# Router parts at the ends of beats, a block list by coded steps, and the last attention beats filled with the shared block

## The chip, the cores and the metric

The kernel runs on one core of a Trainium2 chip. Its five engines are PE (TensorE, matrix products into PSUM banks), DVE (VectorE), ACT (ScalarE), POOL (GpSimd) and SP (SyncE, which here only issues DMAs). They run their own instruction streams in order and wait for each other by semaphores. The metric is device time in microseconds (us), the median of a few executions. PE's clock has two levels here, 1.2 and 2.4 GHz; the profile gives the granted clock as a share of the full one.

## The reference

```python
xn = layernorm(x)                                    # x: 16 batches x 256 tokens x 128
kv = xn @ W_kv; kv = kv * rsqrt(mean(kv**2) + 1e-6) * g_kv;  qc = xn @ W_q
q = concat(heads(qc @ W_qdec), rope(heads(qc @ W_qrope)))    # 16 heads, 8 + 32 wide
k = concat(heads(kv @ W_kdec), rope(heads(xn @ W_krope)))
attn = softmax(where(causal, q @ k.T / sqrt(40), -inf)) @ heads(kv @ W_vdec)
w, e = top2(softmax(xn @ Wg));  w = w / (sum(w) + 1e-9)      # 8 experts
routed = sum_k w_k * (silu(xn @ W1[e_k] + b1[e_k]) @ W2[e_k] + b2[e_k])
shared = silu(xn @ Ws1 + bs1) @ Ws2 + bs2
out = x + attn @ W_o + routed + 0.1 * shared
```

All products are taken in fp32 accuracy: operands are split into a rounded high part and a low rest, and two or three products are summed.

## The kernel before

**Attention.** The 16 batches with 16 heads each make NG = 64 groups, numbered g: four groups for a batch, and in each the query or key side of projections and four heads. The order of everything is written by hand as beats t from -7 to LAST = 71 of four steps s each; (t, s) names a step. In beat t, PE makes the projection of group t (in step 0, `project`); DVE multiplies it by the rope table (L1149, L1156, L1157) in step 1; POOL adds and takes low parts (L761, L766); ACT copies (L945). PE turns parts of group t - 1 and t - 2 (`turn_parted`, L1578) and makes scores for the row maximum of one head in each step (`scores_for_max`, L1593 to L1596), which DVE reduces (`head_max`, L1164). A ring of three PSUM banks (`B_BANKS`) is shared by these scores and turned parts, so PE can't run more than about a step ahead of L1164. The maxima of a group's four heads are turned (L1605), split in a high part (ACT, L928) and a low one (DVE, L1182), and SP copies both into two rows of the operand QK (`place_maxima`, two DMAs of 4 KB, L588) in step (g + 4, 3). Three steps on, the head scores of the group begin (`head_scores`, L1615 to L1618; group 62 in (67, 2), group 63 in (68, 2)); ACT takes exponentials (L914) and PE sums values (`group_values`, L1629, L1632). Each pair of groups is copied out (ACT, L994), turned (L1640), divided by its row sums (DVE, L1190, L1194) into oT; each batch's oT is turned (L1649), copied (ACT, L957), multiplied by W_o (L1660) and added to xres (DVE, L1452).

**Router.** For each quarter q of the tokens, `router(q, part)` runs ten parts on DVE, part 0 to 9, at (16 q + beat, step) of the tables SPREAD (q = 0 to 2) and DENSE (q = 3). Part 4 is L1232 and L1235 on 512 elements for each partition, part 9 begins with L1257. `list_blocks` is a generator: each `next` at a step of LIST_AT issues one piece. It makes the list of the 23 blocks (NB) of 512 routed rows, an expert number and a first row for each (`block_e`, `block_row`, semaphore s_tab), the return places of the tokens' results (`out_at`, s_back) and the chosen biases (`bsel`, s_bsel). POOL scatters the rows to DRAM (L820) up to beat 66.

**Passes.** PASSES are two passes of the shared expert over 512 tokens, 23 routed blocks, then six more shared ones. In pass m PE turns the block (`turn_block`, L1720), makes the hidden layer in four chunks of three products (`hidden`, L1738), and the second layer (`expert_out`, L1802, L1806), and turns the result (L1815). ACT applies Silu (`activate`, L1029) and makes high parts (L1035), DVE low ones (L1480). SP loads weights (L641) and rows (L633) two passes ahead. POOL gathers results (L871) in the late passes and DVE adds them (L1505). Before the first pass SP issues four loads of 512 KB for the shared expert at (66, 0) (`load_shared`).

## Time and profile before

| | |
|---|---|
| median of 3 runs | 718.98 us (717.71 to 720.65) |
| the profiled execution | 720.41 us; its span 718.7 us |
| busy: PE, DVE, ACT, POOL | 652.2, 537.8, 528.6, 430.5 us |
| mean granted PE clock | 0.969 |
| attention beats 0 to 63 | 17.25 to about 465 us |
| last beats | to about 505 us |
| passes | second layer of pass 0 at 518.91 us, the end at 718.7 us |

The span is from the first to the last instruction; the profiled execution's own time is 1.7 us longer. A busy share says how long an engine worked, not that it set the end.

### The profile page before, as it was taken

Reading aid. Unit: us, or ns where it says so; the run is one execution under the profiler, and the core shown is the slowest. Engines: PE = TensorE matmul, PEld = TensorE weight load, DVE = VectorE, ACT = ScalarE, POOL = GpSimd, SP = SyncE. Lnnn points to the kernel's source line nnn. Section 1 sums busy time; section 2 is a strip of 40 time slices with the busy share of each in tenths; the row PEclk is TensorE's granted clock in tenths of the full one; section 3 lists DMA queues with packets and bytes.
Section 4 is the critical chain, followed back from the end, with each engine's and each line's share of the span. In section 5 each row is a group of like instructions: output and inputs, shape, how many; then the busy total and the mean of one; then the engine's idle time right before and its main releaser. Section 6 shows DMA issues by size and latency. Waiting matters only on the chain.

```text
span 718.7 us, 16421 instructions
## 1 busy us (share of the span) xinstructions
PE 652.2 (91%) x5478; PEld 560.2 (78%) x5478; DVE 537.8 (75%) x1327; ACT 528.6 (74%) x1071; POOL 430.5 (60%) x440
## 2 busy tenths in 40 slices
PE   2699989899979999998999999976899999999994
PEld 1588878878868878887888888864688888888883
DVE  6387777686786787777778688788377777788895
ACT  3478868778868778886887888853577777777772
POOL 6677767788887878877687685840000000655773
PEclk9999999999998999998999999988699999999998
DMA  7203113032130321201210000235137777889753
GB/s 194 79 2 105 61 47 105 8 115 65 54 112 7 116 65 54 91 29 42 77 47 32 33 13 21 87 104 204 59 131 222 250 245 247 274 276 291 222 148 85
DMA packets 51953, 79.37 MB, mean 110 GB/s; under 512 B 6289, under 2 KB 31870, under 8 KB 51870
## 3 DMA queue, kind: packets, MB, share of 16 engines
q1 hardware_dynamic: 47198, 69.23, 30.0%
q0 software_dynamic: 4096, 8.40, 4.2%
q8 instruction: 45, 0.74, 0.4%
q10 hardware_dynamic: 576, 0.69, 0.3%
q14 instruction: 38, 0.31, 0.2%
HBM read 47.82 MB, written 29.88 MB: 108 GB/s over the span
## 4 chain that ended last, share of the span: by engine, by line
PE 59%; DVE 14%; POOL 11%; ACT 8%; issue 7%; DMA 1%; POOLq 0%; DVEq 0%; ACTq 0%; SPq 0%
PE bank L1578 6%; PE bank L1802 6%; PE projections L1738 5%; PE bank L1738 5%; PE bank L1629 4%; PE bank L1615 3%; PE bank L1806 3%; POOL QK L871 3%; PE bank L1618 3%; PE bank L1593 2%; PE bank L1596 2%; ACT heads_parted L945 2%; DVE mx L1164 2%; POOL heads_parted L766 2%; ACT QK L920 2%
## 5 line engine op out<-in xcount | busy, mean ns | idle before, releaser
L920 ACT ACTIVATE QK<-bank 120x512 fp32r<-120x512 f32 x256 | 154.9, 606 | 32.7 <-PE bank L1578 27.1
L914 ACT ACTIVATE prob<-bank 128x384 f32<-128x384 f32 x256 | 128.3, 501 | 56.6 <-PE bank L1618 56.4
L871 POOL DMA_INDIRECT QK<-expert_outs,out_at x64 | 67.2, 1050 | 159.4 <-DMA expert_outs<-prob 140.4
L1164 DVE TENSOR_REDUCE mx<-bank 128x3 f32<-128x384 f32 x256 | 140.9, 550 | 22.9 <-PE bank L1596 21.7
L1578 PE MATMUL bank<-identr,heads_parted 128*120 128x128 f32 x1024 | 138.1, 261 | 17.7 <-DVE mx L1164 11.6
L1578 PEld LDWEIGHTS bank<-identr,heads_parted 128*120 128x120 f32 x1024 | 106.6, 141 | 24.6 <-DVE mx L1164 13.6
L766 POOL TENSOR_TENSOR heads_parted<-rot,heads_parted 128x640 fp32r<-128x640 f32 x64 | 101.2, 1581 | 38.1 <-ACT heads_parted L945 37.5
L1480 DVE TENSOR_TENSOR QK<-vaug,QK 128x512 fp32r<-128x512 f32 x124 | 86.4, 698 | 41.6 <-ACT QK L1035 39.2
L761 POOL TENSOR_TENSOR rot<-rot,t 128x512 f32<-128x512 f32 x64 | 82.1, 1283 | 33.7 <-DVE t L1157 33.6
L1593 PE MATMUL bank<-QK 120*128 120x256 f32 x256 | 94.8, 370 | 4.8 <-DVE mx L1164 3.0
L1615 PE MATMUL bank<-QK 122*128 122x256 f32 x256 | 90.7, 355 | 3.5 <-DMA QK<-mT 3.4
L945 ACT ACTIVATE heads_parted<-rot 128x1280 fp32r<-128x1280 f32 x64 | 82.3, 1286 | 1.6 <-POOL rot L761 1.5
L820 POOL DMA_INDIRECT expert_rows<-xn,place_of x64 | 65.5, 1023 | 25.2 <-issue 9.9
L1149 DVE TENSOR_TENSOR rot<-projections,rope_table 128x640 f32<-128x640 f32 x64 | 52.6, 822 | 36.0 <-PE projections L1566 28.5
L1618 PE MATMUL bank<-identb,mask_qk 128*128 128x256 bf16 x256 | 74.3, 290 | 0.0
L1596 PE MATMUL bank<-mask_qk,identb 128*128 128x256 bf16 x256 | 74.3, 290 | 0.0
L1594 PE MATMUL bank<-QK 120*128 120x128 f32 x256 | 57.8, 226 | 0.0
L1616 PE MATMUL bank<-QK 122*128 122x128 f32 x256 | 57.7, 225 | 0.0
L1593 PEld LDWEIGHTS bank<-QK 120*128 120x128 f32 x256 | 52.8, 206 | 6.2 <-DVE mx L1164 3.3
L1615 PEld LDWEIGHTS bank<-QK 122*128 122x128 f32 x256 | 49.5, 193 | 6.0 <-DMA QK<-mT 3.7
L1594 PEld LDWEIGHTS bank<-QK 120*128 120x128 f32 x256 | 50.5, 197 | 0.0
L1616 PEld LDWEIGHTS bank<-QK 122*128 122x128 f32 x256 | 50.2, 196 | 0.0
(226 smaller groups left out, 1582.0 us busy)
## 6 DMA issues: line engine op xcount, KB each, us to landing
wb<-weight_parts SPq DMA_DIRECT2D x46, 512.0 KB, 4.8
weight_parts<-wb SPq DMA_DIRECT2D x18, 512.0 KB, 3.4
rot<-expert_rows SPq DMA_DIRECT2D x23, 256.0 KB, 4.3
expert_outs<-prob SPq DMA_DIRECT2D x23, 256.0 KB, 4.8
xn<-in_L_ffn_W SPq DMA_DIRECT2D x16, 256.0 KB, 4.0
xn_parts<-wb SPq DMA_DIRECT2D x16, 256.0 KB, 2.8
heads_parted<-xn_parts SPq DMA_DIRECT2D x8, 512.0 KB, 4.5
expert_rows<-zeros SPq DMA_DIRECT2D x15, 256.0 KB, 2.8
```

The lines of the kernel that those rows point to most:

```text
L766: nc.gpsimd.tensor_tensor(low_of(g), rotated(g), high_of(g)[:, :, 0:D], ALU.subtract).then_inc(s_lo, 1)
L871: nc.gpsimd.indirect_dma_start(out=gy[:, t, k, :], out_offset=None, in_=outs_d[0:READY[q] * SLOTS, :], in_offset=bass.IndirectOffsetOnAxis ...
L914: act_f(prob[:, g % 2 * HG + n, :], ST_PS[n % 2][:, 0:3 * P], ACT.Exp, scale=SCALE).then_inc(s_exp, 1)
L920: act_f(stacked(g, i), B_PS[bank_of(k)][0:KQ, :].rearrange("p (h t) -> p h t", h=HG), ACT.Copy)\
L945: act_f(high_of(g).rearrange("p m (a d) -> p m a d", a=2), rotated(g).unsqueeze(2).to_broadcast([P, NT * PH, 2, D]), ACT.Copy).then_inc(s_ ...
L1164: V.tensor_reduce(mx[:, g % 2, 0:3, n], B_PS[bank_of(k)][:, 0:3 * P].rearrange("p (a c) -> p a c", a=3), AX.X, ALU.max, negate=True).then_ ...
L1578: ins = nc.tensor.transpose(B_PS[bank_of(k)][0:KQ, n * P:(n + 1) * P].bitcast(F32R), parted(g)[:, j * PH + 2 * n + odd, :], identr[:, :])
L1593: mm(ps[:, 0:T], q[:, P:T], kk, start=True, stop=False, skip_group_check=True)
L1594: mm(ps[:, T:3 * P], q[:, 0:P], kk[:, 0:P], start=False, stop=False, skip_group_check=True)
L1615: mm(ps[:, P:3 * P], k[:, 0:P], q, start=True, stop=False, skip_group_check=True)
L1616: mm(ps[:, 0:P], k[:, P:T], q[:, P:T], start=False, stop=False, skip_group_check=True)
L1618: mm(diag, mask_qk[:, :], identb[:, :].unsqueeze(1).to_broadcast([P, 2, P]), start=False, stop=True, skip_group_check=True).then_inc(s_st, 1)
```

## The change

- SPREAD puts seven of the ten router parts at the last step of a beat. Part 4 moves from (12, 0) to (13, 3), counted from the quarter's first beat, part 9 from (19, 0) to (18, 3).
- The block list no longer selects a segment by equality and sums two products. Expert number times 65536 plus shift is one code for each segment; the steps between the codes of neighbours are summed over all segments that a block has passed, and the expert number is the count of multiples of 65536 that the sum reaches. LIST_AT has 10 entries for 21, from (61, 3) to (68, 3).
- The return places come last in the generator and are issued in passes 3 to 10 (BACK_AT). The biases come ahead of them.
- The shared block's first hidden layer stands in four places of the last beats, (68, 0), (68, 1), (69, 1), (69, 2), and two chunks of the second pass behind the beats. The values of group 62 move from (69, 0) to (68, 1). The last batch's turning and output product leave the beats and use bank 7, with copies and addition on DVE; the last pair's copy moves from ACT to DVE.
- ACT calls Silu on two elements behind its last beat and then waits for the last values.
- SP issues the loads of weights for the first two routed blocks behind all maxima, and after each block's rows.

```diff
--- before.py
+++ after.py
@@ -117,7 +117,9 @@
-    if s == 0 and group(t - 7) and (t - 7) % 2 == 0:
+    if (t, s) == (LAST - 3, 1):
+        return NG - 2
+    if s == 0 and group(t - 7) and (t - 7) % 2 == 0 and t - 7 < NG - 2:
...
@@ -181,11 +183,12 @@
-SPREAD = ((8, 3), (10, 3), (11, 0), (11, 3), (12, 0), (12, 2), (14, 3), (16, 3), (18, 3), (19, 0))
+SPREAD = ((8, 3), (10, 3), (11, 3), (12, 3), (13, 3), (14, 2), (14, 3), (16, 3), (17, 3), (18, 3))
-LIST_AT = ((62, 3), (63, 3), (64, 0), (64, 1), (64, 2), (64, 3), (65, 0), (65, 1), (65, 2), (65, 3), (66, 0), (66, 1),
-           (66, 2), (66, 3), (67, 0), (67, 1), (67, 2), (68, 0), (68, 1), (68, 2), (69, 2))
+LIST_AT = ((61, 3), (62, 3), (63, 3), (64, 3), (65, 3), (66, 3), (67, 1), (67, 3), (68, 1), (68, 3))
+BACK_AT = (3, 4, 5, 6, 7, 8, 9, 10)
+CODE = 65536
...
@@ -662,13 +668,9 @@
-                if t in (67, 68) and s == 0:
-                    if t == 67:
-                        sp.wait_ge(s_tab, 1)
-                        sp.wait_ge(s_pfill, NG)
-                    for part in range(2):
-                        load_weights(t - 67, part)
+            sp.wait_ge(s_tab, 1)
+            sp.wait_ge(s_pfill, NG)
...
@@ -676,6 +678,8 @@
+                for part in range(2):
+                    load_weights(r_, part)
...
@@ -951,7 +955,7 @@
-                if s == 2 and out_batch(t) is not None:
+                if s == 2 and out_batch(t) in range(B - 1):
...
@@ -987,7 +991,7 @@
-                if s == 3 and pair_at(t) is not None:
+                if s == 3 and pair_at(t) in range(NG // 2 - 1):
...
@@ -1041,6 +1045,8 @@
+            act_f(warm[:, :], mhalf[:, :], ACT.Silu).then_inc(s_table, 1)
+            sc.wait_ge(s_pv, NG)
...
@@ -1336,31 +1344,44 @@
+                steps.add(V.scalar_tensor_tensor(out=coded, in0=expert_no[:, :], scalar=float(CODE), in1=shift, op0=ALU.mult,
+                                                 op1=ALU.add))
+                steps.add(V.tensor_tensor(leap, coded[:, 1:SEGS + 1], coded[:, 0:SEGS], ALU.subtract))
-                steps.add(V.tensor_tensor(sel[:, :, 0:SEGS], by_block(block_no, SEGS), each(flat2(end), SEGS), ALU.is_ge))
+                steps.add(V.tensor_tensor(sel, by_block(block_no, SEGS), each(flat2(end), SEGS), ALU.is_ge))
-                steps.add(V.tensor_reduce(seg, sel[:, :, 0:SEGS], AX.X, ALU.add))
+                steps.add(V.tensor_tensor(sel, sel, each(leap, SEGS), ALU.mult))
-                steps.add(V.tensor_tensor(sel, by_block(seg, SEGS + 1), each(seg_no[:, :], SEGS + 1), ALU.is_equal))
+                steps.add(V.tensor_reduce(code, sel, AX.X, ALU.add))
-                steps.add(V.tensor_tensor(val, sel, each(expert_no[:, :], SEGS + 1), ALU.mult))
+                steps.add(V.scalar_tensor_tensor(out=code, in0=block_no, scalar=float(SLOTS), in1=code, op0=ALU.mult, op1=ALU.add))
+                steps.add(V.tensor_tensor(bound, by_block(code, E - 1), each(code_of[:, :], E - 1), ALU.is_ge))
+                steps.add(V.tensor_reduce(no, bound, AX.X, ALU.add))
+                steps.add(V.tensor_copy(block_e[:, :], no))
+                steps.add(V.scalar_tensor_tensor(out=row, in0=no, scalar=-float(CODE), in1=code, op0=ALU.mult, op1=ALU.add))
+                steps.add(V.tensor_tensor(chosen, by_block(no, E), each(seg_no[:, 0:E], E), ALU.is_equal))
+                V.tensor_copy(block_row[:, :], row).then_inc(s_tab, 1)
-                steps.add(V.tensor_tensor(sel, sel, each(shift, SEGS + 1), ALU.mult))
+                steps.add(V.tensor_tensor(parts, chosen.unsqueeze(2).to_broadcast([P, NB, FC, E]),
+                                          bias[:, 0:E * FC].rearrange("p (e c) -> p c e", c=FC).unsqueeze(1)
+                                          .to_broadcast([P, NB, FC, E]), ALU.mult))
-                steps.add(V.tensor_reduce(no, val, AX.X, ALU.add))
-                steps.add(V.tensor_reduce(row, sel, AX.X, ALU.add))
-                steps.add(V.tensor_copy(block_e[:, :], no))
-                steps.add(V.scalar_tensor_tensor(out=row, in0=block_no, scalar=float(SLOTS), in1=row, op0=ALU.mult, op1=ALU.add))
-                steps.add(V.tensor_tensor(chosen, by_block(no, E), each(seg_no[:, 0:E], E), ALU.is_equal))
-                V.tensor_copy(block_row[:, :], row).then_inc(s_tab, 1)
+                steps.add(V.tensor_tensor(second, chosen, each(bias[:, NE * FC:NE * FC + E], E), ALU.mult))
+                dve.wait_ge(s_sc[GROUPS - 1], 16 * 2 * GT)
+                steps.add(V.tensor_reduce(bsel[:, :, 0:FC], parts, AX.X, ALU.add))
+                V.tensor_reduce(bsel[:, :, FC:FC + 1], second.unsqueeze(2), AX.X, ALU.add).then_inc(s_bsel, 1)
...
@@ -1439,12 +1450,16 @@
+                if s == 3 and pair_at(t) == NG // 2 - 1:
+                    dve.wait_ge(s_pv, NG)
+                    dve.wait_ge(s_bk, NG // 2 - 1)
+                    V.tensor_copy(heads_out[:, :], PV_PS[:, 0:T]).then_inc(s_ev, 1)
-                if s == 0 and added_batch(t) is not None:
+                if s == 0 and added_batch(t) in range(B - 1):
...
@@ -1458,6 +1473,11 @@
+            dve.wait_ge(s_lfill, 1)
+            V.tensor_copy(oT[:, :], banks[7][:, 0:T]).then_inc(s_lread, 1)
+            dve.wait_ge(s_lfill, 2)
+            V.tensor_tensor(xres[:, TILES - NT:TILES, :], banks[7][:, T:2 * T].rearrange("p (j c) -> p j c", j=NT),
+                            xres[:, TILES - NT:TILES, :], ALU.add).then_inc(s_lread, 1)
...
@@ -1515,6 +1535,8 @@
+                if m in BACK_AT:
+                    next(listing, None)
...
@@ -1758,6 +1780,8 @@
+                if (t, s) == (LAST - 3, 1):
+                    hidden(0, (1,))
...
@@ -1767,7 +1791,7 @@
-                if s == 1 and out_batch(t) is not None:
+                if s == 1 and out_batch(t) in range(B - 1):
...
@@ -1778,17 +1802,28 @@
-                if s == 3 and out_batch(t) is not None:
+                if s == 3 and out_batch(t) in range(B - 1):
-                if (t, s) == (LAST - 2, 3):
+                if (t, s) == (LAST - 3, 0):
-                    hidden(0, range(0, 2))
-            ring_empty(pe)
-            hidden(0, range(2, FC))
-            pe.wait_ge(s_exp, H * B)
+                    hidden(0, (0,))
+                if (t, s) == (LAST - 2, 1):
+                    ring_empty(pe)
+                    hidden(0, (2,))
+                if (t, s) == (LAST - 2, 2):
+                    hidden(0, (3,))
+            hidden(1, (0,))
+            for j in range(NT):
+                ins = nc.tensor.transpose(banks[7][:, j * P:(j + 1) * P], oT[:, j * P:(j + 1) * P], ident[:, :])
+            ins.then_inc(s_lfill, 1)
+            hidden(1, (1,))
+            pe.wait_ge(s_lread, 1)
+            for j in range(NT):
+                ins = mm(banks[7][:, T + j * P:T + (j + 1) * P], oT[:, j * P:(j + 1) * P], wo[:, :], start=True, stop=True)
+            ins.then_inc(s_lfill, 1)
...
@@ -1811,13 +1846,15 @@
+                if m == 0:
+                    pe.wait_ge(s_lread, 2)
-                hidden(m + 1)
+                hidden(m + 1, range(FC) if m else range(2, FC))

...
```

On DVE around beats 12 to 14, before (quarter 0; `tables` are the comparison tables, `rot` the rope product):

```order
L1229 TENSOR_TENSOR tables<-pr 128x512
L1164 TENSOR_REDUCE mx<-bank 128x3
L1190 RECIPROCAL inv_sum<-bank 128x16
L1194 TENSOR_TENSOR oT<-bank,inv_sum 128x2x64
L1232 TENSOR_TENSOR tables<-tables,tri 128x512
L1235 TENSOR_TENSOR tables<-tables 128x512
L1149 TENSOR_TENSOR rot<-projections,rope_table 128x640
L1164 TENSOR_REDUCE mx<-bank 128x3
```

and of the change, from beat 13's turned rope products on:

```order
L1164 TENSOR_TENSOR t_1<-projections,rope_table 128x16x16
L1171 TENSOR_REDUCE mx<-bank 128x3
L1189 TENSOR_TENSOR mT<-bank,mT 4x256
L1171 TENSOR_REDUCE mx<-bank 128x3
L1239 TENSOR_TENSOR tables<-tables,tri 128x512
L1242 TENSOR_TENSOR tables<-tables 128x512
L1171 TENSOR_REDUCE mx<-bank 128x3
L1197 RECIPROCAL inv_sum<-bank 128x16
L1201 TENSOR_TENSOR oT<-bank,inv_sum 128x2x64
L1156 TENSOR_TENSOR rot<-projections,rope_table 128x640
L1171 TENSOR_REDUCE mx<-bank 128x3
```

The pair of `tables` operations (L1232 and L1235, in the change L1239 and L1242) left the place ahead of the rope multiply and stands between two row maxima.

On PE from the last head scores of group 63, at (69, 1), to the second layer of pass 0, before:

```order
L1618 MATMUL bank<-identb,mask_qk 128x256
L1629 MATMUL bank<-prob,vaug 32x256 x4
L1632 MATMUL bank<-prob,vaug 32x128 x4
L1738 MATMUL projections<-heads_parted 128x512 x6
L1640 MATMUL bank<-ident,heads_out 128x128 x2
L1649 MATMUL bank<-ident,oT 128x128 x2
L1660 MATMUL bank<-wo,oT 128x128 x2
L1738 MATMUL bank<-heads_parted 128x512 x6
L1720 MATMUL bank<-ident,rot 128x128 x4
L1738 MATMUL projections<-heads_parted 128x512 x6
L1738 MATMUL bank<-heads_parted 128x512 x6
L1802 MATMUL bank<-QK,heads_parted 128x512 x8
```

and of the change (L1760 is `hidden`, L1651 and L1654 the values), from (68, 0) on:

```order
L1662 MATMUL bank<-ident,heads_out 128x128 x2
L1760 MATMUL projections<-heads_parted 128x512 x3
L1637 MATMUL bank<-QK 128x256
L1638 MATMUL bank<-QK 128x128
L1640 MATMUL bank<-identb,mask_qk 128x256
L1760 MATMUL projections<-heads_parted 128x512 x3
L1651 MATMUL bank<-prob,vaug 32x256 x4
L1654 MATMUL bank<-prob,vaug 32x128 x4
```

and further on, from the last head scores of group 63 at (69, 1):

```order
L1640 MATMUL bank<-identb,mask_qk 128x256
L1760 MATMUL bank<-heads_parted 128x512 x3
L1651 MATMUL bank<-prob,vaug 32x256 x4
L1654 MATMUL bank<-prob,vaug 32x128 x4
L1760 MATMUL bank<-heads_parted 128x512 x3
L1662 MATMUL bank<-ident,heads_out 128x128 x2
L1760 MATMUL projections<-heads_parted 128x512 x3
L1820 MATMUL bank<-ident,oT 128x128 x2
L1760 MATMUL projections<-heads_parted 128x512 x3
L1825 MATMUL bank<-wo,oT 128x128 x2
L1742 MATMUL bank<-ident,rot 128x128 x4
L1760 MATMUL bank<-heads_parted 128x512 x6
```

The hidden layer's twelve products stood behind the beats, six of them behind W_o; now three stand ahead of each of four waits.

On SP, the maxima and what is issued around them, before:

```order
L588 DMA QK<-mT 1x4x256 x2
L626 DMA heads_parted<-weight_parts 128x1024
L616 DMA heads_parted<-xn_parts 128x2x512
L626 DMA heads_parted<-weight_parts 128x1024
L616 DMA heads_parted<-xn_parts 128x2x512
L588 DMA QK<-mT 1x4x256 x2
L638 TENSOR_LOAD block_e
L638 ISA x2
L641 ISA
L641 DMA wb_0<-weight_parts 128x1024
```

and of the change:

```order
L594 DMA QK<-mT 1x4x256 x2
L632 DMA heads_parted<-weight_parts 128x1024
L622 DMA heads_parted<-xn_parts 128x2x512
L632 DMA heads_parted<-weight_parts 128x1024
L622 DMA heads_parted<-xn_parts 128x2x512
L594 DMA QK<-mT 1x4x256 x4
L638 TENSOR_LOAD block_row
L638 ISA x2
L639 ISA
L639 DMA rot<-expert_rows 128x512
```

The four loads of the shared block stand at the same place ahead of group 62's maxima; the weights (`wb`) that stood between the two groups' maxima now follow both.

## Rows read from the trace of the kernel before

**Rows 1.** The page's busy times and shares of the span by engine.

```profile
PE 652.2 (91%) x5478; PEld 560.2 (78%) x5478; DVE 537.8 (75%) x1327; ACT 528.6 (74%) x1071; POOL 430.5 (60%) x440
```

**Rows 2.** Waits of PE, 36 to 470 us: total us, times, longest.

```profile
PE bank L1578 <- DVE mx L1164: 11.6, 6, 3.6
```

**Rows 3.** Timeline of PE, first projections of beats: start, us, instruction.

```profile
91.07 0.39 PE L1557 MATMUL projections<-wqa,qsT 128*128 128x320 f32 x1
101.86 0.39 PE L1562 MATMUL projections<-wkr,wb 128*128 128x256 f32 x1
...
180.08 0.39 PE L1557 MATMUL projections<-wqa,qsT 128*128 128x320 f32 x1
186.87 0.39 PE L1562 MATMUL projections<-wkr,wb 128*128 128x256 f32 x1
...
207.27 0.39 PE L1557 MATMUL projections<-wqa,qsT 128*128 128x320 f32 x1
220.00 0.39 PE L1562 MATMUL projections<-wkr,wb 128*128 128x256 f32 x1
...
324.58 0.39 PE L1557 MATMUL projections<-wqa,qsT 128*128 128x320 f32 x1
336.21 0.39 PE L1562 MATMUL projections<-wkr,wb 128*128 128x256 f32 x1
```

**Rows 4.** Line L1232 (ns min/median/max), and L1235 in the timeline of DVE.

```profile
L1232 DVE TENSOR_TENSOR tables<-tables,tri x4: 414/1474/2436, 92.8 to 432.6; 128x512 bf16<-128x512 bf16 x4
...
94.33 0.55 DVE L1235 TENSOR_TENSOR tables<-tables 128x512 bf16<-128x512 bf16 x1
```

**Rows 5.** Line L1257, same form.

```profile
L1257 DVE TENSOR_SCALAR rsm<-rsm x4: 159/1056/1514, 145.5 to 451.7; 128x8 f32<-128x8 f32 x4
```

**Rows 6.** Timeline of DVE and of POOL at the end of beat 13.

```profile
107.02 0.54 DVE L1164 TENSOR_REDUCE mx<-bank 128x3 f32<-128x384 f32 x1
...
109.66 1.55 POOL L766 TENSOR_TENSOR heads_parted<-rot,heads_parted 128x640 fp32r<-128x640 f32 x1 [2.25 <-ACT heads_parted L945]
```

**Rows 7.** Groups of DVE, 455 to 512 us: busy us, mean ns, idle before.

```profile
L1380 DVE TENSOR_TENSOR xn<-xn 128x1024 f32<-128x1024 f32 x2 | 2.4, 1216 | 0.0
...
L1332 DVE TENSOR_TENSOR xn<-xn 128x32 f32<-128x32 f32 x1 | 2.0, 1972 | 0.0
...
L1349 DVE TENSOR_TENSOR xn<-xn,expert_no 128x759 f32<-128x759 f32 x1 | 0.9, 940 | 0.0
```

**Rows 8.** Windows: PE, PEld, DVE, ACT, POOL busy; granted clock, DMA share, GB/s.

```profile
470.20:483.10 12.90, 10.68 (x92) 9.04 (x91) 10.39 (x19) 6.07 (x15) 4.99 (x5) 0.74 0.27 85
483.10:492.90 9.80, 5.34 (x50) 3.96 (x48) 9.32 (x23) 2.93 (x7) 0.00 (x0) 1.00 0.68 229
...
492.90:499.40 6.50, 3.65 (x37) 2.70 (x37) 6.08 (x12) 2.43 (x6) 0.00 (x0) 1.00 0.43 154
499.40:516.50 17.10, 14.57 (x68) 9.63 (x67) 5.50 (x11) 8.04 (x14) 0.00 (x0) 0.50 0.29 92
516.50:518.90 2.40, 2.40 (x11) 1.96 (x11) 2.08 (x4) 2.03 (x5) 0.00 (x0) 1.00 0.33 107
```

**Rows 9.** Timeline of SP's queue (issues merged) and of PE at the head scores.

```profile
483.12 0.35 SPq L626 DMA_DIRECT2D heads_parted<-weight_parts  x1
...
487.82 2.45 SPq L588 DMA_DIRECT2D QK<-mT  x2
...
495.10 2.58 SPq L588 DMA_DIRECT2D QK<-mT  x2
...
492.94 0.39 PE L1615 MATMUL bank<-QK 122*128 122x256 f32 x1 [1.10 <-DMA QK<-mT]
...
498.83 0.38 PE L1615 MATMUL bank<-QK 122*128 122x256 f32 x1 [2.26 <-DMA QK<-mT]
```

**Rows 10.** Timeline of ACT, the load of Silu's table.

```profile
510.48 1.28 ACT L1029 ACT_TABLE_LOAD   x1
```

**Rows 11.** Window of a late pass with sums of results on DVE.

```profile
641.30:647.80 6.50, 6.50 (x33) 5.33 (x33) 5.75 (x12) 4.88 (x10) 4.98 (x6) 1.00 0.89 258
```

31 lines of the change are left out of this document (15 added, 16 removed).

## The prediction

> **What bounds the kernel now.** I read the busy shares of the page first: PE (TensorE) is busy for 91% of the span and every other engine for 75% or less [rows 1]. So PE must be late for a reason wherever it stands still, and what is to be found is where it stands. From 519 us on it never does. One window of the expert passes shows PE busy 6.50 of 6.50 us at the full clock, while DVE (VectorE) has 0.75 us to spare even with sums of routed results in it [rows 11]. Nothing that only moves work on other engines speeds these 200 us up. In the attention stage the waits of PE name one releaser above all: 11.6 us in 6 waits of the transposes L1578 for the row maxima of DVE (L1164) [rows 2]. I then took the start of each beat's projection as a ruler. A beat with t divisible by 4 takes 6.79 us (180.08 to 186.87); beats 12, 28 and 44 take 10.79, 12.73 and 11.63 us [rows 3]. In these three, and there alone, router part 4 stands ahead of the rope multiply and of a row maximum. Last I cut the end of the attention stage in stretches [rows 8]: from 470.2 to 483.1 the clock averages 0.74, from 483.1 to 492.9 PE works 5.34 of 9.8 us, and from 499.4 to 516.5 it runs at the half level throughout.
>
> **Router parts.** In beat 12 DVE runs L1232 from 92.8 and L1235 (0.55 us) from 94.33; over its four calls L1232 takes 0.41 to 2.44 us, 1.47 in the median [rows 4]. The stall that follows lets the clock fall to the half level, so the beats lose more than the operations last. If all of this goes, the gain is 10.79 + 12.73 + 11.63 - 3 x 6.79 = 14.8 us. Where the two go, after the row maximum of step 3 in beats 13, 29 and 45: in beat 13 that maximum ends at 107.56 and POOL (GpSimd) has been idle for 2.25 us when it starts at 109.66 [rows 6]. With the free duration of 0.41 and 0.55 us they end at 108.5. The bank that the next maximum frees is wanted by PE only after its projection, so I take a remaining loss of 0.5 us for each of the three beats, 1.5 us. From below this is 0; from above it is the 2.44 us form instead of the 0.41 in each, 3 x 2.03 + 1.5 = 7.6 us.
>
> What makes the long form: the records of L1257, on eight elements of each partition, also spread from 0.16 to 1.51 us [rows 5], and that can't be work; a wait lies inside them, and I take it to be one on POOL. The Trainium skill, SBUF — State Buffer, section "SBUF: two separate sides", says that DVE and GpSimd share a port pair as an exclusive lock, and that a DVE operation with two SBUF inputs waits out a GpSimd operation that reads SBUF. The spread agrees with it. By that rule the indirect DMAs of POOL (about 1 us each), too, could hold the operation in beat 45, which adds 0.7 us to the sum; the bound above covers that.
>
> The tiny part 9 (L1257) takes 1.06 us in the median and 0.16 at best [rows 5]. It moves from step 0 to the step before it. The beats that follow have odd numbers, in which PE does values and a projection before DVE is wanted. I count 3 x 0.9 = 2.7 us gained; at least 0. Against that, the first piece of the block list moves from (62, 3) to (61, 3), behind part 9 and ahead of an even beat: 0.6 us lost, its free duration. Router balance: 14.8 - 1.5 + 2.7 - 0.6 = 15.4 us.
>
> **Block list.** One selection over 32 segments, one product and one sum remain of it; four operations like L1349 (0.94 us) on the DVE queue go and small ones come. The return places, six operations like L1380 (1.22 us), leave the last beats for passes 3 to 10 [rows 7]. In the passes they stand behind the previous result's copy. The window that already has 1 us of extra DVE work shows PE full [rows 11], so I cost them at nothing; their cover is DVE's idle time in a pass of 6.5 us, and if it is gone the price is at most 8 x 0.5 = 4 us. In the beats, L1332 (1.97 us) delays a maximum and PE stands 2.2 us at 470.2; it moves one step pair on, behind a maximum. The PE work between 470.2 and 483.1 is 10.68 us, of which the clock (mean 0.74, so 6.7 us at the half level) accounts for 3.35; 7.3 us remain. With 1.2 us for waits on POOL's last low parts and for the maxima's way to SP I put the shared block's loads 8.5 us after 470.2 where they now are 12.9 us after it (483.12): gain 4.4 us.
>
> **What is late next.** This is the step on which most hangs. SP issues four loads of 512 KB at 483.12 and then, at 487.82, the two 4 KB copies of the maxima of group 62. The second is issued by 490.27, and the head scores that want it start at 492.94, 2.67 us later. For group 63 that interval is 498.83 - 497.68 = 1.15 us, with no large transfer directly ahead [rows 9]. So the small copy waits behind the 2 MB. From the first load to the scores it takes 9.82 us, and the change leaves these transfers and their order alone. PE's own work in between is 5.34 us [rows 8]. Faster beats therefore only make PE wait about 4.5 us at (67, 2); the gain up to here stays 4.4 us. The Trainium skill, DMA: Bandwidth & Descriptors, section "Queues, rings and completion order", says that descriptors are consumed in ring order; this trace agrees, by the 1.5 us of difference.
>
> **Last beats and shared block.** From 492.9 to 518.9 PE's busy time is 3.65 at the full clock, 14.57 at the half level and 2.40 at full: 3.65 + 7.29 + 2.40 = 13.3 us of full-speed work in 26.0 us [rows 8]. The change leaves this work as it is but fills the waits with chunks of the shared block: chunk 0 and 1 stand between the scores of group 62, chunk 2 and 3 around the last values, and two chunks of the second shared pass before and behind the last transposes. The last copies of batch 15 go to DVE. The Silu table (1.28 us at 510.48 [rows 10]) is loaded during the last values instead of ahead of the first activation. The weights of r0 and r1 no longer stand ahead of group 63's maxima; they are issued behind the beats, about 10 us before pass 2 wants the first of them, for 512 KB each where four such loads took some 8 us. I add 1.2 us for waits (probabilities of the last head, DVE copy and norm) and, since PE has stood still for 4.5 us, 2.5 us for a half-level spell like the 6.7 us one at 472 (at most 3.4). New length 17.0 us, gain 9.0 us.
>
> A page prices this differently. The Trainium skill, ScalarE: Activation LUTs, section "What ACT_TABLE_LOAD costs", gives about 2.66 us for a switch with its drain. By it the first activation would come 1.4 us later and the sum be 7.6 us; here the whole load is one record of 1.28 us, so the row decides.
>
> **Sum.** The profiled execution took 720.41 us (span 718.7 and 1.7 around it), 1.43 above the median of 718.98. 720.41 - 15.4 - 4.4 - 9.0 = 691.6; on the scale of the median 690.2. I forecast **690 us**.
>
> **Rivals.** (A) The stalls of part 4 move with it: POOL or a full DVE queue holds beats 14, 30 and 46 as it holds 12, 28 and 44. For it: those beats are even ones, with little DVE slack. Against: POOL is idle at 107.56. Price 7.6 - 1.5 plus the clock spells (3 x 1.5) = 10.6 us: 701 us. (B) The small copies do not queue behind the loads, so there is no wait at (67, 2) and no half-level spell: 4.5 + 2.5 us better, 683 us. Against it stands the 2.67 against 1.15 us. (C) The filling fails: chunk 0 of the shared block waits for its loads and holds up the in-order scores behind it, or the half level lasts through the last beats again. All 13.3 us at the half level give 26.6 instead of 17.0 us: 700 us. (D) Slower than before: the clock stays at the half level behind the wait at (67, 2) and on through the expert passes, where PE has no slack. A pass of 6.5 us would take up to 13, so the 28.8 us are used up after 4.5 such passes. From 519 us on the present trace shows the full clock in a stretch of this density, against it. (E) The filling does nothing for the end but the router parts do: about 699 us.
>
> **How the numbers follow.** Forecast 0.55 (685 to 695), A 0.13, B 0.12, C and E 0.15, D 0.02, something unnamed with small effect 0.03. The range from 681 to 702 takes in A, B, C and E with 1 us beyond. Faster by over 0.5% (3.6 us, about what a measurement of this kernel can tell from no change) 0.95, within it 0.03, slower 0.02.
>
> **What would show it.** Right: beats 12, 28 and 44 near 6.8 us and no clock fall there; beats 14, 30 and 46 under 8.5 us; head scores of group 62 waiting some 4 us for the maxima's DMA; expert_out(0) about 17 us behind them; passes of 6.47 us. Wrong: a half level in beats 13 to 14, PE waiting in front of the shared block's first chunk, or passes 3 to 10 longer than those behind them.

## The result, and the profile after

The changed kernel takes **694.0 us** (median of 4 runs, 692.33 to 694.69) against 718.49 us for the kernel before (717.71 to 720.65), a ratio of 0.9649 with the 95% interval 0.9624 to 0.9675. The forecast was 690 us. (The 718.98 us in the table of before is the median of its first three runs, 718.49 us that of four.) The profiled execution took 693.57 us with a span of 691.8.

In what follows lines of after stand some 5 to 40 higher than those of before for the same code: the transposes for the maxima L1578 are L1600 now, the row maximum L1164 is L1171, the head scores L1615 are L1637, the SP copies of the maxima L588 are L594, the shared loads L626 are L632, the first expert result is L1837; the kernels of the experiments differ from that by up to 11 lines. And of the ten router parts nine, not seven, stand at the last step of a beat in the new table; six did in the old one.

The page's busy times of after, to be held against [rows 1]: PE has 11.8 us less to do (less time at the half level) in a span that is 26.9 us shorter.

```profile
PE 640.4 (93%) x5478; PEld 550.8 (80%) x5478; DVE 524.9 (76%) x1331; ACT 527.1 (76%) x1070; POOL 428.4 (62%) x440
```

The waits of PE between 36 and 450 us (total, times, longest). The six waits of 11.6 us in [rows 2] are 1.9 us in four, and nothing has come in their place that is longer than 1.2 us.

```profile
PE projections L1701 <- DVE t L1164: 4.6, 14, 0.4
...
PE bank L1600 <- DVE mx L1171: 1.9, 4, 0.5
PE bank L1600 <- POOL heads_parted L770: 1.2, 1, 1.2
```

Timeline of PE, first projections of beats 12, 13 and 14 in after. Beat 12 takes 99.29 - 91.80 = 7.49 us, not 10.79 as in [rows 3].

```profile
91.80 0.39 PE L1579 MATMUL projections<-wqa,qsT 128*128 128x320 f32 x1
...
99.29 0.39 PE L1584 MATMUL projections<-wkr,wb 128*128 128x256 f32 x1
...
105.72 0.39 PE L1579 MATMUL projections<-wqa,qsT 128*128 128x320 f32 x1
```

Router part 4's product, formerly up to 2.44 us long [rows 4], in after (ns min/median/max). In the three quarters whose place was changed it took 1.48, 2.44 and 1.47 us before and takes 0.77, 0.76 and 0.97 us in after, so it became shorter but not the 0.41 us that the prediction set for it.

```profile
L1239 DVE TENSOR_TENSOR tables<-tables,tri x4: 416/768/968, 104.9 to 419.7; 128x512 bf16<-128x512 bf16 x4
```

What it waits for inside its record can be read beside POOL's rows. In before, quarter 0:

```profile
92.44 1.56 POOL L766 TENSOR_TENSOR heads_parted<-rot,heads_parted 128x640 fp32r<-128x640 f32 x1
92.81 1.48 DVE L1232 TENSOR_TENSOR tables<-tables,tri 128x512 bf16<-128x512 bf16 x1
```

and in after:

```profile
104.12 1.28 POOL L765 TENSOR_TENSOR rot<-rot,t 128x512 f32<-128x512 f32 x1
104.92 0.77 DVE L1239 TENSOR_TENSOR tables<-tables,tri 128x512 bf16<-128x512 bf16 x1
```

POOL's operation ends at 94.00 and DVE's at 94.29; POOL's at 105.40 and DVE's at 105.69. In all six cases of the two kernels DVE's record ends 0.28 to 0.29 us behind that of POOL's L766 (before) or L765 (after). So the wait is one on POOL, as the prediction took it to be, but POOL is not idle at the new place: it works on its next rope sum there, and only 0.3 to 0.6 us are lost instead of 1.1 to 2.0.

Timeline of PE at the end of the attention stage: the transposes of oT for batch 14, the first head scores of group 62 (the square bracket is PE's wait ahead of them), the first expert result.

```profile
467.50 0.44 PE L1671 MATMUL bank<-ident,oT 128*128 128x128 f32 x2 [1.07 <-DVE oT L1201]
...
475.00 0.58 PE L1637 MATMUL bank<-QK 122*128 122x256 f32 x1 [2.83 <-DMA QK<-mT]
...
491.81 2.18 PE L1837 MATMUL bank<-QK,heads_parted 128*128 128x512 f32 x8
```

Windows of the same stretch (PE, PEld, DVE, ACT, POOL busy; granted clock, DMA share, GB/s). They answer to [rows 8]. PE stands still ahead of 475.10, then 5.2 us pass at the half level (1.2 GHz), and from 480.3 the clock is full; in before the half level lasted from 499.4 to 516.5.

```profile
466.30:475.10 8.80, 4.90 (x51) 3.99 (x49) 6.41 (x15) 2.92 (x7) 0.00 (x0) 0.93 0.72 233
475.10:480.30 5.20, 4.90 (x31) 3.37 (x32) 1.77 (x9) 2.01 (x5) 0.00 (x0) 0.50 0.08 29
480.30:491.90 11.60, 11.21 (x84) 8.16 (x83) 6.46 (x15) 8.27 (x15) 0.00 (x0) 0.99 0.69 225
```

SP's queue in after, issues merged; this answers to [rows 9]. The first shared load goes out at 466.33, 8.67 us ahead of the scores at 475.00 (9.82 us before), and the copies for group 62 start to go out at 469.20.

```profile
466.33 0.35 SPq L632 DMA_DIRECT2D heads_parted<-weight_parts  x1
...
469.20 10.30 SPq L594 DMA_DIRECT2D QK<-mT  x4
```

From the first expert result to the end it is 691.8 - 491.81 = 200.0 us, and 718.7 - 518.91 = 199.8 us in before: the passes gave nothing and took nothing.

### The profile page after: what moved, and what is told of

Its sections match the earlier page's. It is cut to its first block, busy times and chain, and to the rows that moved or that the text cites. A ratio compares the mean times of both kernels' runs of the same rounds, so it can differ in the third digit from the quotient of the medians.

```text
span 691.8 us, 16437 instructions
## 1 busy us (share of the span) xinstructions
PE 640.4 (93%) x5478; PEld 550.8 (80%) x5478; DVE 524.9 (76%) x1331; ACT 527.1 (76%) x1070; POOL 428.4 (62%) x440
## 4 chain that ended last, share of the span: by engine, by line
PE 66%; DVE 11%; POOL 8%; ACT 6%; issue 6%; DMA 1%; POOLq 0%; DVEq 0%; ACTq 0%; SPq 0%
PE bank L1600 7%; PE bank L1837 7%; PE projections L1760 6%; PE bank L1760 5%; PE bank L1651 5%; PE bank L1637 4%; PE bank L1841 3%; PE bank L1615 3%; PE bank L1640 3%; PE bank L1618 3%; POOL QK L875 2%; PE projections L1584 2%; PE bank L1654 2%; PE bank L1627 2%; DVE mx L1171 2%
## 5 line engine op out<-in xcount | busy, mean ns | idle before, releaser
L1171 DVE TENSOR_REDUCE mx<-bank 128x3 f32<-128x384 f32 x256 | 140.9, 550 | 20.0 <-PE bank L1618 18.6
L1600 PE MATMUL bank<-identr,heads_parted 128*120 128x128 f32 x1024 | 136.0, 258 | 8.2 <-POOL heads_parted L770 4.3
L1600 PEld LDWEIGHTS bank<-identr,heads_parted 128*120 128x120 f32 x1024 | 104.9, 139 | 14.7 <-POOL heads_parted L770 5.5
L765 POOL TENSOR_TENSOR rot<-rot,t 128x512 f32<-128x512 f32 x64 | 82.2, 1285 | 26.0 <-DVE t L1164 25.8
L1615 PE MATMUL bank<-QK 120*128 120x256 f32 x256 | 93.3, 364 | 3.1 <-DVE mx L1171 2.3
L1637 PE MATMUL bank<-QK 122*128 122x256 f32 x256 | 89.5, 350 | 3.1 <-DMA QK<-mT 2.8
L824 POOL DMA_INDIRECT expert_rows<-xn,place_of x64 | 65.0, 1015 | 21.3 <-issue 10.1
L1615 PEld LDWEIGHTS bank<-QK 120*128 120x128 f32 x256 | 51.6, 202 | 4.9 <-ACT QK L924 3.3
L1637 PEld LDWEIGHTS bank<-QK 122*128 122x128 f32 x256 | 48.7, 190 | 5.1 <-DMA QK<-mT 3.0
L1616 PEld LDWEIGHTS bank<-QK 120*128 120x128 f32 x256 | 49.5, 193 | 0.0
L1189 DVE TENSOR_TENSOR mT<-bank,mT 4x256 fp32r<-4x256 f32 x64 | 26.4, 412 | 30.3 <-ACT mT L932 29.9
```

What stands on the lines that cost most here:

```text
L1171: V.tensor_reduce(mx[:, g % 2, 0:3, n], B_PS[bank_of(k)][:, 0:3 * P].rearrange("p (a c) -> p a c", a=3), AX.X, ALU.max, negate=True).then_ ...
L1600: ins = nc.tensor.transpose(B_PS[bank_of(k)][0:KQ, n * P:(n + 1) * P].bitcast(F32R), parted(g)[:, j * PH + 2 * n + odd, :], identr[:, :])
L1615: mm(ps[:, 0:T], q[:, P:T], kk, start=True, stop=False, skip_group_check=True)
L1616: mm(ps[:, T:3 * P], q[:, 0:P], kk[:, 0:P], start=False, stop=False, skip_group_check=True)
L1637: mm(ps[:, P:3 * P], k[:, 0:P], q, start=True, stop=False, skip_group_check=True)
```

## The experiments

**How they are read.** The experiments ran in three sets of four, each set on a chip of its own. There the kernel before takes 733.63, 739.65 and 735.77 us instead of 718.49, with single runs of one kernel up to 1.5% apart, so these chips are taken to be others than that of the first two profiles. The kernel before was not profiled there. In the changed kernel run again most of the extra time lies in the last passes: between 640 and 700 us PE is busy for 47.0 of 60 us at a mean granted clock of 0.89, where it was always busy up to 680 us in the first profile. Two of its waits there, for DVE's sums of gathered rows and for ACT, in the timeline:

```profile
684.16 1.08 PE L1852 MATMUL bank<-ident,prob 128*128 128x128 f32 x4 [4.91 <-DVE xres L1514]
689.82 1.62 PE L1760 MATMUL projections<-heads_parted 128*128 128x512 f32 x3 [4.57 <-ACT vaug L1033]
```

What lies before them hardly differs. Beats 5 to 60 repeat to 0.15 us apart from beat 41 (6.65 to 6.87 us), and passes 1 to 15 to 0.03 us, where no edit touches them. Only beats 2 to 4, in which the clock rises for the first time, differ, together by up to 2.1 us and without a pattern, and beats 61 and 62 together take 1.6 to 3.2 us more than in the first profiles. So the verdicts rest on stretches of the profile, one profile for each kernel, and the times stand beside them. Three rulers, all in us, from the timelines of PE and of SP: **A**, the start of beat 62's projection; **B**, from the start of beat 63's to the first shared load; **C**, from the oT transposes of batch 14 (the row at 467.50 above) to the first expert result; and the wait of PE for the maxima of group 62. A ruler has a scatter of its own. B is 18.64, 19.1 or 20.7 us in kernels that don't differ up to there; at 20.7 the clock fell to the half level on the way (mean 0.92 in the changed kernel run again, 1.00 in the first profile). C is 22.92 to 25.43 us in five kernels whose last beats are the same (changed twice, old places, odd slots, return places dense), as the wait for group 62 is 2.4 to 4.2 us and the mean clock over C 0.93 (at 22.92) or 0.86 to 0.87.

| kernel | time, ratio to before | A | B | C | wait for group 62 |
|---|---|---|---|---|---|
| before | 718.49 | 452.84 | 22.83 | 34.38 | 1.10 |
| changed | 694.0, 0.9649 [0.9624, 0.9675] | 440.00 | 18.64 | 24.31 | 2.83 |
| changed, again (second set) | 709.32, 0.958 [0.9516, 0.9643] | 440.40 | 20.74 | 24.73 | 2.88 |
| before + new places of the parts | 725.0, 0.986 [0.9785, 0.9936] | 440.05 | 22.85 | 34.39 | 1.19 |
| changed, old places | 725.04, 0.9851 [0.9776, 0.9927] | 455.41 | 19.11 | 25.43 | 4.17 |
| no filling | 713.28, 0.9703 [0.9637, 0.9769] | 440.75 | 19.11 | 28.29 | 4.75 |
| split loads | 704.61, 0.9589 [0.9507, 0.967] | 438.51 | 19.13 | 19.31 | none |
| maxima on ACT's queue | 717.63, 0.9702 [0.9611, 0.9794] | 440.96 | 20.73 | 23.75 | 2.50 |
| odd slots | 706.67, 0.955 [0.9473, 0.9628] | 436.34 | 20.66 | 25.43 | 3.82 |
| weights early | 716.66, 0.9689 [0.9608, 0.977] | 440.38 | 19.19 | 28.11 | 2.51 |
| dense list | 710.86, 0.9656 [0.9615, 0.9697] | 439.15 | 24.25 | 23.29 | 0.56 |
| return places dense | 708.62, 0.9626 [0.9562, 0.9689] | 440.40 | 19.11 | 22.92 | 2.40 |
| table late | 708.0, 0.9617 [0.9575, 0.9659] | 440.72 | 19.10 | 24.87 | 3.20 |
| split loads + odd slots | 698.42, 0.9464 [0.9415, 0.9513] | 436.87 | 19.13 | 19.40 | none |

By the times alone the new places and the old places in the changed kernel are unclear at 2% (both intervals lie below 1), all others are faster than before. Of the kernels with one edit in the changed one only that with the old places has an interval apart from those of the changed kernel.

**The changed kernel again.** No edit.

> The changed kernel itself, as the measure on the chip of this set of runs. Expected: its ratio to the kernel before is again 0.965, beats and the end part as in its first profile to 0.1 us, save for the waits for transfers, which took up to 2 us longer on the chip of the first four runs.

The ratio is 0.958, on a slower chip; beats 5 to 60 agree with the first profile but for beat 41. That only waits for transfers differ was wrong: in beat 62 (9.60 instead of 7.69 us) PE waits 1.1 us for a row maximum of DVE, 0.5 us in the first profile, and the mean granted clock of the beat is 0.82 instead of 1.00. Why that is so on these chips stays open.

**The new places alone.** The kernel before with one line changed:

```diff
-SPREAD = ((8, 3), (10, 3), (11, 0), (11, 3), (12, 0), (12, 2), (14, 3), (16, 3), (18, 3), (19, 0))
+SPREAD = ((8, 3), (10, 3), (11, 3), (12, 3), (13, 3), (14, 2), (14, 3), (16, 3), (17, 3), (18, 3))
```

> The kernel before with the new table of places of the router parts and nothing else. Theory (the router term of the sum, as the traces of before and after now give it): beats 12, 28 and 44 lose their 12.6 us, beats 14, 30 and 46 gain 1.8 us, beats 19, 35 and 51 lose 3.6 us, so the start of beat 62's projection comes about 13 us earlier and the time is about 705 us. Rival: part of these beats' gain belongs to the list of blocks or to the end; then the time is 709 us or more. Rival 2: with the parts moved but the end left as before, the expert passes or the last beats absorb some of it (a transfer that sets the end); then the beats are shorter but the time is above 709 us.

Ruler A falls from 452.84 to 440.05, as in the changed kernel (440.00), and beats 5 to 60 are those of the changed kernel, with beats 6 and 41 0.1 us longer. B and C stay those of before. The router term stands alone and is worth 12.8 us of a profile; the ratio of 0.986 is 10.3 us of that chip's 733.63, with an interval from 4.7 to 15.8.

**The old places in the changed kernel.** The same line the other way round.

> The changed kernel with the old table of places of the router parts, all else as changed. If the terms add: 694 + 13 = 707 us, the parts' waits back in beats 12, 28 and 44 (10.8 to 12.7 us each), the end part unchanged at about 44 us from beat 62 to the first expert result. If the router's places and the end interact (the clock at the end, the POOL queue), the time is under 704 or over 710 us.

Ruler A goes to 455.41, back by 15.4 us from the kernel with the new places alone, where 13 were expected; beats 12, 28 and 44 take 11.07, 13.12 and 11.93 us, a little longer still than in before. B and C are those of a changed kernel. So the two halves of the change add, within 2 us.

**No filling.** The four chunks of the first shared pass behind the beats, those of the second behind the last projection:

```diff
-                if (t, s) == (LAST - 3, 0):
-                    pe.wait_ge(s_turned, NG)
-                    pe.wait_ge(s_v, NG)
-                    hidden(0, (0,))
-                if (t, s) == (LAST - 2, 1):
-                    ring_empty(pe)
-                    hidden(0, (2,))
-                if (t, s) == (LAST - 2, 2):
-                    hidden(0, (3,))
-
-            hidden(1, (0,))
+            ring_empty(pe)
+            pe.wait_ge(s_turned, NG)
+            pe.wait_ge(s_v, NG)
+            hidden(0)
```

(and likewise `hidden(0, (1,))` out of beat LAST - 3, `hidden(1, (1,))` behind the last projection.)

> The changed kernel with all four chunks of the first shared pass behind the beats, and both chunks of the second one behind the last projection, as before; the Silu table, the last copies on DVE, the list and the loads stay changed. Theory: the filling itself is most of the 9 us of the last term, so the stretch from the first head scores of group 62 to the first expert result grows from 17 to 23 to 26 us, with a half level in it, and the time is 700 to 703 us. Rival: the gain came from the table load, the copies and the last values' earlier place; then the time is 695 to 697 us.

PE in this kernel at the transposes, at the scores and at the first expert result:

```profile
469.56 0.44 PE L1671 MATMUL bank<-ident,oT 128*128 128x128 f32 x2 [1.07 <-DVE oT L1201]
...
479.00 0.58 PE L1637 MATMUL bank<-QK 122*128 122x256 f32 x1 [4.75 <-DMA QK<-mT]
...
497.85 0.84 PE L1828 MATMUL bank<-QK,heads_parted 128*128 128x512 f32 x3
```

From the scores to the first expert result 18.85 us, where 23 to 26 were expected and the changed kernel has 16.81. Ruler C is 2.9 us longer than in the kernel with the old places, on the same chip (28.29 against 25.43), and that is above its scatter. The filling is worth about 3 us, a third of the last term and not most of it. The ratio of 0.9703 is 697 us of 718.49, at the upper end of the rival's 695 to 697. The rest of the term lies in what this kernel keeps.

**Weights early.** The four loads of 512 KB for the first two routed blocks again ahead of group 63's maxima:

```diff
+                if t in (67, 68) and s == 0:
+                    if t == 67:
+                        sp.wait_ge(s_tab, 1)
+                        sp.wait_ge(s_pfill, NG)
+                    for part in range(2):
+                        load_weights(t - 67, part)
...
-                for part in range(2):
-                    load_weights(r_, part)
```

> The changed kernel with the weight loads of the first two routed blocks (four of 512 KB) back at beats 67 and 68, ahead of the maxima of group 63 on SP's queue. Theory (small copies behind large ones in a queue are late): the head scores of group 63 wait some 2 us for their maxima again, as they did in the kernel before (2.26 us), perhaps with a half-level spell of the clock, so the stretch from the head scores of group 62 to the first expert result grows from 16.8 to 19 to 22 us. Rival: the shared block's chunks stand in that place now and hide it; then it grows by less than 1 us.

PE in this kernel:

```profile
476.50 0.39 PE L1639 MATMUL bank<-QK 122*128 122x256 f32 x1 [2.51 <-DMA QK<-mT]
486.45 0.58 PE L1639 MATMUL bank<-QK 122*128 122x256 f32 x1 [4.13 <-DMA QK<-mT]
```

The second line is group 63, which waits 4.13 us for its maxima (2.26 in before, [rows 9]; no such wait in the changed kernel) and then runs at the half level. Ruler C grows from 24.73 to 28.11, by 3.4 us; from scores to expert result it is 20.93 us, within the 19 to 22 expected. But the expected reason, small copies behind large ones, is not the one that the trace shows. DVE's part of the maxima and its last operation of the block list, then SP's queue:

```profile
478.69 0.41 DVE L1191 TENSOR_TENSOR mT<-bank,mT 4x256 fp32r<-4x256 f32 x1 [2.90 <-ACT mT L934]
...
480.50 0.18 DVE L1375 CAST block_row<-xn 128x23 int32<-128x23 f32 x1
```

```profile
481.62 1.50 SPq L647 DMA_DIRECT2D wb<-weight_parts  x2
483.23 1.29 SPq L594 DMA_DIRECT2D QK<-mT  x2
```

The maxima are ready at 479.10, and their copies are issued from 483.23 on. SP stands still until the list is written (`sp.wait_ge(s_tab, 1)`, 8.3 us in all), because in the new schedule the list is ready only behind group 63's maxima; in before it was ready at 486.09, ahead of group 62's. So this experiment shows that the weights had to move once the list had moved. It doesn't show that their move shortened anything against before, and the 3.4 us are no part of the gain. There the second copy for group 63 waited for DVE's low part, and DVE had two operations of the return places ahead of it, while ACT's high part was ready at 495.07:

```profile
495.40 1.23 DVE L1384 TENSOR_TENSOR xn<-xn 128x1024 f32<-128x1024 f32 x1
496.66 0.41 DVE L1182 TENSOR_TENSOR mT<-bank,mT 4x256 fp32r<-4x256 f32 x1
```

The second copy went out at 497.10, when the low part was ready, and the scores started at 498.83. The return places so account for up to 1.6 of the 2.26 us.

**Dense list.** All pieces of the list in the beats, in the first 18 of the old places; none in the passes:

```diff
-LIST_AT = ((61, 3), (62, 3), (63, 3), (64, 3), (65, 3), (66, 3), (67, 1), (67, 3), (68, 1), (68, 3))
-BACK_AT = (3, 4, 5, 6, 7, 8, 9, 10)
+LIST_AT = ((62, 3), (63, 3), (64, 0), (64, 1), (64, 2), (64, 3), (65, 0), (65, 1), (65, 2), (65, 3), (66, 0), (66, 1), (66, 2), (66, 3), (67, 0), (67, 1), (67, 2), (68, 0))
+BACK_AT = ()
```

> The changed kernel with all 18 pieces of the list, the return places among them, in the first 18 of the places that the kernel before used at the end of the beats; nothing of it in the passes. Theory (DVE has no slack in the last beats, and this is the 4.4 us of the sum): the shared block's loads are issued 3 to 5 us later after the start of beat 63 than in the changed kernel on the same chip, with a wait of PE for a row maximum of 2 us or more on the way. Rival: the gain of the loads' issue came from elsewhere (POOL, the clock), and it moves by less than 1 us. With coded steps the list is 4 long operations shorter than in the kernel before, so it may lie at the lower end.

PE in this kernel:

```profile
461.90 0.58 PE L1615 MATMUL bank<-QK 120*128 120x256 f32 x1 [2.39 <-DVE mx L1171]
475.44 0.44 PE L1671 MATMUL bank<-ident,oT 128*128 128x128 f32 x2 [2.31 <-DVE oT L1201]
```

The wait for a row maximum is back (2.39 us; 2.22 us at 472.46 in before), and B is 24.25 against 19.11 and 19.10 in the two kernels below from the same chip: 5.1 us, part of it by the clock (mean 0.86 over B, 1.00 in the kernel with the late table). The places, not the coded steps, carry the term; coded steps in the old places leave B even above the 22.83 of before. From beat 63 to the first expert result it is 49.58 us against 45.13 and 43.21 in these two: the list's places are worth 4.5 to 6.4 us there. All of that lies up to the oT transposes: C is 23.29 us, no longer than the 24.87 and 22.92 of the two.

**Return places dense.** Two pieces in pass 3, two in pass 4, four in pass 5:

```diff
-BACK_AT = (3, 4, 5, 6, 7, 8, 9, 10)
+BACK_AT = (3, 3, 4, 4, 5, 5, 5, 5)
...
-                if m in BACK_AT:
+                for _ in range(BACK_AT.count(m)):
                     next(listing, None)
```

> The changed kernel with the eight pieces of the return places in three passes instead of eight: two in pass 3, two in pass 4 and four in pass 5. Theory (they cost nothing because DVE is idle for about 1 us or more of each pass): one piece of 1.2 us fits, so passes 3 and 4 with two pieces (2.4 us) grow by 0 to 1 us and pass 5 with four (4.9 us) by 2 to 4 us over 6.47; the remaining passes are 6.47. Rival: DVE's work has more room than its busy share says because PE works from two buffers; then all three stay at 6.5 us. Either way the passes without a piece keep 6.47, which says that one piece per pass cost nothing.

DVE in the pass with four pieces, from the first to the last of them: five operations, 4.1 us long.

```profile
530.20 1.22 DVE L1401 TENSOR_TENSOR xn<-xn 128x1024 f32<-128x1024 f32 x1
...
534.23 0.20 DVE L1413 CAST out_at<-xn 128x64 uint32<-128x64 f32 x1
```

The two passes with two pieces keep 6.47 us, the one with four takes 6.80. I had expected 2 to 4 us more for it, so the rival is nearer. One piece in a pass lies far from where DVE decides.

**Table late.** Without the early activation:

```diff
-            act_f(warm[:, :], mhalf[:, :], ACT.Silu).then_inc(s_table, 1)
             sc.wait_ge(s_pv, NG)
```

> The changed kernel without the early activation that loads the Silu table during the last values; the load stands ahead of the first activation of the shared block, as in the kernel before, and the wait for the last values stays. Theory: the load of 1.28 us then lies behind the first chunk and the activations, which run one behind the other in front of the first expert result, all come later: 0.3 to 1.3 us more between the last oT transposes and the first expert result. Rival: ACT stands at the wait for the last values anyway and the table was already loading in that time; no change within 0.2 us.

ACT in this kernel: the last probabilities, the load, the first Silu.

```profile
487.23 0.87 ACT L918 ACTIVATE prob<-bank 128x384 f32<-128x384 f32 x2 [0.28 <-PE bank L1639]
488.12 1.28 ACT L1033 ACT_TABLE_LOAD   x1
489.42 1.26 ACT L1033 ACTIVATE vaug<-projections,bias 128x512 f32<-128x512 f32 x2
```

In the changed kernel the load stands at the same place, 0.01 us behind the last exponential:

```profile
485.44 1.28 ACT L1048 ACT_TABLE_LOAD   x1
```

With or without the early activation it follows the last exponential at once, and the first Silu comes 1.30 us behind the start of the load here and 1.41 us behind it (486.85) in the changed kernel. C is 24.87, within its scatter. The rival is right: the early activation is worth nothing.

**Split loads.** Only the first half of the 2 MB goes out ahead of group 62's maxima:

```diff
                     load_shared(0)
-                    load_shared(1)
+                if g == NG - 2:
+                    load_shared(1)
```

(at g = 62 that is right behind the two copies of the maxima; the second weights have a semaphore of their own, and PE waits for it at the first expert result.)

> The changed kernel with the second weights and the second input chunk of the shared block issued behind the maxima of group 62 instead of ahead of them, and PE waiting for the second weights only at the first expert result. Theory (the small copies wait in their queue behind the 2 MB): half of the bytes stand ahead, so the copies land 4 us earlier, the wait of 2.83 us at (67, 2) goes and with it the half-level spell of 6 us that follows it: 694 - 2.8 - 2 to 3 = 688 to 689 us. Rival 1 (the copies share the bandwidth with whatever large transfers are under way, in no order): the second megabyte now comes just behind them, the wait stays at 2 us or more and the time within 1 us of 694. Rival 2: the wait goes, but the maxima of group 63 or the second input chunk are late instead: the wait moves to (68, 2) or to the second shared pass and the time is 692 to 696 us.

PE in this kernel at the transposes, the scores of group 62 and the first expert result; then SP's queue; then a window from the transposes to the expert result:

```profile
469.00 0.44 PE L1673 MATMUL bank<-ident,oT 128*128 128x128 f32 x2 [1.07 <-DVE oT L1203]
...
473.44 0.36 PE L1639 MATMUL bank<-QK 122*128 122x256 f32 x1
...
488.31 1.95 PE L1841 MATMUL bank<-QK,heads_parted 128*128 128x512 f32 x7
```

```profile
467.84 0.33 SPq L633 DMA_DIRECT2D heads_parted<-weight_parts  x1
...
470.71 1.23 SPq L595 DMA_DIRECT2D QK<-mT  x2
471.99 0.43 SPq L633 DMA_DIRECT2D heads_parted<-weight_parts  x1
```

```profile
469.00:488.30 19.30, 18.30 (x160) 14.00 (x161) 13.43 (x33) 12.69 (x26) 0.00 (x0) 1.00 0.71 238
```

The scores start at 473.44 without a wait, at most 1.5 us behind the issue of the second copy (470.71 + 1.23 = 471.94), and the clock stays at 1.00. Ruler C is 19.31 against 25.43 in the kernel with the old places on the same chip, 6.1 us less; against the first profile's 24.31 it is 5.0. That is as the theory had it (4.8 to 5.8 us), and nothing turns up late in its stead up to the first expert result. The time doesn't resolve it: the ratio of 0.9589 [0.9507, 0.967] overlaps both of the changed kernel. But this experiment can't tell whether the queue or the bytes under way made the copies late.

**Maxima on ACT's queue.** Group 62's two copies are issued by ACT, the four loads stay where they are:

```diff
                 if g is not None:
                     put_max(g)
+                if g == NG - 2:
+                    for part in range(2):
+                        ...
+                        sc.dma_start(QK[KQ + part:KQ + part + 1, g // PER % 2, 0, heads_of(g), :].bitcast(F32),
+                                     mT[part][:, g % 2, :].bitcast(F32)).then_inc(s_mrow[g % 2], 16)
```

> The changed kernel with the two 4 KB copies of group 62's maxima issued by ACT, behind its own copy of the high parts, instead of by SP; the four loads of 512 KB stay ahead of them in time on SP's queue. Theory (what made them late is their place behind 2 MB in one queue): on a queue of their own they land within some 2 us of their issue although the same 2 MB is under way; the wait for them at (67, 2), 2.8 to 4.8 us so far, falls to under 0.7 us and the clock stays at full there. Rival (the copies share the engines with the bulk, whichever queue they are in): the wait stays at 2 us or more. In either case PE loses up to 1 us more elsewhere because ACT waits for DVE's low parts ahead of the next exponential, and the first two chunks of the shared block now wait for their loads, so the time may gain less than the 4.4 us of the split.

The page of this kernel shows that they did change the queue: q10 carries 592 packets instead of 576, and q1, SP's, 47182 instead of 47198.

Timeline of this kernel: the first load, the copies, the scores.

```profile
471.34 0.35 SPq L632 DMA_DIRECT2D heads_parted<-weight_parts  x1
...
474.22 1.82 ACTq L972 DMA_DIRECT2D QK<-mT  x2
...
480.06 0.58 PE L1646 MATMUL bank<-QK 122*128 122x256 f32 x1 [2.50 <-DMA QK<-mT]
```

The rival is right. From the first load to the scores it is 480.06 - 471.34 = 8.72 us on a queue of their own, and 479.47 - 470.74 = 8.73 us in the changed kernel on the same chip, although the copies are issued later here. That the two agree to 0.01 us is luck: the same stretch takes 8.25 to 10.61 us in the other kernels that issue 2 MB ahead. What counts is that the copies did not land within some 2 us of their issue. The packets of the queues, in the window from 478.3 to 479.6 us and in that from the scores to 482.5 us:

```profile
q10 hardware_dynamic: 16, 0.01, 2.1%
```

```profile
q1 hardware_dynamic: 100, 0.19, 19.8%
```

All 16 packets of the two copies on ACT's queue lie in the first window, and none between their issue at 474.22 and 478.3. So the data itself starts late. But it doesn't wait for the end of the 2 MB: 0.19 MB of the loads are still moved behind 480.06, when the scores already read what the copies brought. The Trainium skill, DMA: Bandwidth & Descriptors, section "Queues, rings and completion order", says that the semaphore increment "lands only after every earlier write from that SDMA engine, across its queues". The late packets show that something else made these copies late, since their data already was; whether the increments waited too, no run here shows. By what rule the packets of a second queue are held back behind a bulk load stays open.

**Odd slots.** Three parts moved from ahead of an even beat to ahead of an odd one:

```diff
-SPREAD = ((8, 3), (10, 3), (11, 3), (12, 3), (13, 3), (14, 2), (14, 3), (16, 3), (17, 3), (18, 3))
+SPREAD = ((8, 3), (10, 3), (10, 3), (12, 3), (12, 3), (14, 2), (14, 3), (16, 3), (18, 3), (18, 3))
```

> The changed kernel with router parts 2, 4 and 8 moved from the step ahead of an even beat to a step ahead of an odd beat, (10, 3), (12, 3) and (18, 3), where they stand behind parts 1, 3 and ahead of part 9. Theory (an odd beat has slack for DVE, since PE does the values and a projection before it wants DVE; an even beat has none): beats 12, 28 and 44 go from 7.5 to 6.8 us, beats 14, 30 and 46 from 8.05 to 7.5 us or less (7.5 is what they take in the kernel before), beat 50 from 8.05 to 7.5, and the odd beats stay at 6.44: 3 to 4 us less than the changed kernel. Rival (the work costs PE the same wherever it stands, or two parts in one slot exceed the slack): beats 11, 13, 27, 29, 43, 45 grow by 0.5 to 1 us each and the time is within 1 us of the changed kernel, or above it.

First projections of beats 12 to 15 in this kernel: 6.79, 6.87 and 7.51 us, where the changed kernel beside it has 7.50, 6.44 and 8.03.

```profile
90.41 0.39 PE L1579 MATMUL projections<-wqa,qsT 128*128 128x320 f32 x1
...
97.20 0.39 PE L1584 MATMUL projections<-wkr,wb 128*128 128x256 f32 x1
...
104.07 0.39 PE L1579 MATMUL projections<-wqa,qsT 128*128 128x320 f32 x1
...
111.58 0.39 PE L1584 MATMUL projections<-wkr,wb 128*128 128x256 f32 x1
```

Even beats give back 2.2 us in beats 12, 28 and 44, 1.8 us in 14, 30 and 46 and 0.9 us in 18, 34, 50 and 55; the odd beats 13, 29 and 45 take 1.4 us of it, since part 4 now shares a slot with part 3. That is 3.5 us net, within the 3 to 4 expected (ruler A moves by 4.06, of which 0.7 is the chance of beats 2 to 4). The ratio's interval [0.9473, 0.9628] overlaps that of the changed kernel. The slack of odd beats is real and not large.

**Both.** The two edits that gained, together (their diffs are above).

> Both edits that gained, together: the second weights and input chunk of the shared block issued behind group 62's maxima, and router parts 2, 4 and 8 ahead of odd beats. If they add (4.1 us in the beats, 5 to 6 us in the end part): beat 62's projection at 436.3 and the first expert result at 484 to 485 us, 9 to 10 us earlier than in the changed kernel, the time 684 to 686 us where no transfer holds the last passes; against the changed kernel's ratio of 0.965 to 0.958 this is 0.945 to 0.952. Rival: earlier beats meet the gathers and fills on the way and part of it is lost again: the first expert result at 487 us or later.

The first expert result starts at 487.06, against 491.81 in the first profile of the changed kernel and 496.64 on a chip like this one. I expected 484 to 485; beats 61 and 62, longer on these chips, account for the difference (7.18 and 10.50 us against 6.83 and 7.69). A and C keep what each edit gave alone, and the mean granted clock over C is 1.00 in both kernels with split loads. The ratio to before is 0.9464, with an interval (0.9415 to 0.9513) that lies below both intervals of the changed kernel (0.9516 is the lower end of the nearer one), though measured on another chip. By the ratios it is 1.2 to 1.9% below the changed kernel. Against either edit alone the intervals overlap.

## Why the prediction was right, and where its steps were not

The time is 4 us above the forecast, and the profiled execution 2.0 us above the sum of 691.6. The terms did less well than their sum.

**Router parts.** 15.4 us foretold, 12.6 measured (beat 63 starts at 447.69 instead of 460.29). The step that was mis-sized is "if all of this goes": beats 12, 28 and 44 fell to 7.49, 7.54 and 7.51 us and not to 6.79, because the new table puts part 2 ahead of beats 12, 28 and 44, and an even beat has no slack for it. That is 2.2 us. The new loss in beats 14, 30 and 46 was put at 1.5 us and is 1.8; beats 19, 35 and 51 gave 3.6 us where 2.7 were counted; the first piece of the list cost beat 62 0.24 us and not 0.6; beat 50 lost 0.55 us to part 8, which the sum didn't have, and beats 3 and 4 lost 0.7 by the chance of the clock's first rise. The kernel with odd slots shows the cause: without parts ahead of even beats these are 6.8 and 7.5 us again. POOL was not idle at the new place, as [rows 6] had let the prediction expect; that cost 0.3 to 0.6 us of DVE's time and none of PE's, since beats 13, 29 and 45 keep 6.44 us. The indirect DMAs of POOL, which the prediction feared, hold nothing in this case: `tables<-is,pr` on 128 elements, with two inputs too, starts at 376.33 inside one of them (376.25 to 377.20) in before and takes 0.28 us, its shortest time. Rival A is out: no beat of the three passes 8.3 us and the clock stays full.

**Block list.** 4.4 us foretold, 4.2 measured to the first shared load (18.64 against 22.83 us from beat 63; 2.1 to 3.7 us in the later profiles, where B is 19.1 to 20.7), and the dense list shows that its places carry it. That the return places cost nothing in the passes holds with much room.

**What is late next.** That PE would wait for group 62's maxima once the beats are faster was right in kind: 2.83 us instead of 4.5, since load to scores took 8.67 and not 9.82 us. The reason given was half right. "The small copy waits behind the 2 MB" was meant as a place in SP's queue. With half of the bytes ahead the copies are in time, so the bulk ahead is the cause; but on another queue they were as late, so the queue is not, nor do they wait for its last bytes. The half-level spell of 5.2 us cost about 4.90 / 2 = 2.5 us, as costed. Rival B, that small copies don't queue behind the loads, is out, but its price of 7 us was near what the split gives back (5.0 to 6.1).

**Last beats.** 17.0 us foretold, 16.8 measured; the gain of 9.0 is 26.0 - 16.8 = 9.2. Here the number was right and its reason is shown for a third only, so that this term came out is in part luck. The prediction gave the gain to the filling. Of the 10.1 us by ruler C (34.38 to 24.31) the filling, taken out singly, is worth 2.9; the early table nothing; the places of the list nothing within C. About 7 us have no owner. What the trace shows of them is the clock: over C PE is busy for 25.82 us at a mean clock of 0.75 in before and for 20.79 us at 0.86 in the changed kernel, for the same work, so 5.0 of the 10.1 us are PE's own slower pace, in the half-level spell of [rows 8] from 499.4 to 516.5. No edit brought that spell back: without the filling PE is busy for 20.3 us over C, with the weights early for 20.9. The earlier values of group 62, the last batch's own bank and the last copies on DVE were not tried alone, nor two edits together. Of the wait of 2.26 us for group 63's maxima up to 1.6 us were the return places ahead of their low part on DVE; the prediction counted what their move gives only up to the shared loads.

**Passes.** 6.47 us in all of passes 3 to 10, as foretold; rival D is out.

## What to carry to other kernels

Issue a bulk load behind the small transfer that the next instructions want, and split it by the time when each part is wanted; another queue doesn't help. Before adding work to an engine with no slack, look for the stretches in which its consumer has other work first: the same router parts cost up to 5.9 us a beat, 0.7 us or nothing, by their place alone. When several edits share a stretch, take each out once, and read in the trace what the kernel then waits for: the filling was a third of the gain here, and the weights that were put back made PE wait for a list that other lines had moved. Look where an issuing engine blocks, since what stands behind the block in its program is late too.

## What the runs showed of the hardware

- Two 4 KB copies on a queue of their own were used no sooner than on the queue of the 2 MB issued ahead of them: 8.72 against 8.73 us from the first load (8.25 to 10.61 in other kernels with the loads ahead). Their first packet came at least 4.08 us behind the start of their issue (474.22 to 478.3), and their last before the last 0.19 MB of the 2 MB. With 1 MB ahead and 1 MB right behind, they were there at most 1.5 us after their issue.
- A DVE product with two inputs of 128x512 took 0.41 us at its shortest and 0.76 to 2.44 us beside POOL's operations on 128x640 and 128x512; in all six such cases of the two first profiles it ended 0.28 to 0.29 us behind POOL's. A product with two inputs of 128 elements kept its 0.28 us inside an indirect DMA of POOL.
- The load of the activation table started right behind the last exponential whether or not an activation was put there for it (0.01 and 0.02 us behind it), took 1.28 us, and the next activation came 0.02 us behind it.
- The changed kernel repeats beats 5 to 60 to 0.15 us (beat 41 to 0.2) between the first profile and that of the second set, while its whole time differs by 15 us, 694.0 and 709.3 us. The two profiled executions differ by 20.5 us of span: 4.8 us lie ahead of the first expert result, nearly all of that in beats 61 and 62 and up to the shared loads, and the rest in the last passes, in waits (one of 4.91 us above) and at a lower granted clock.
